# The first context tile in halves, the first weights one by one, the identity on ScalarE's queue, and twelve transposes on TensorE while it waits

## The chip, the core and the metric

The kernel runs on one core of a Trainium2 chip. A core has a matrix engine (TensorE, PE in the profile), VectorE (DVE), ScalarE (ACT), GpSimd (POOL) and SyncE (SP), which here only issues transfers; 16 DMA engines carry these. The metric is the time of one execution on the device in microseconds, as the median of several runs. The kernel before takes 2266.22 us (three runs: 2265.88, 2266.22, 2270.08).

## What is computed

One transformer layer on x [8, 256, 1024] and a context ctx [8, 256, 1024], in float32: cross attention with 32 query heads, 8 key and value heads and a rotary embedding, then a feed-forward product whose 4-bit weights are unpacked and scaled.

```python
q = rope(layernorm(x) @ Wq)                 # 32 heads of 128
k, v = rope(ctx @ Wk), ctx @ Wv             # 8 heads of 128, repeated 4 times
attn = softmax(where(mask == 0, -1e9, q @ k.T / sqrt(128)))
x = x + (attn @ v) @ Wo
x = x + layernorm(x) @ dequantize(qweight, qzeros, scales) + bias
```

## The kernel before

**Products in parts.** Each float32 operand is split into a high part (a copy rounded to the matmul's format, made by ScalarE) and a low part (operand minus high part, made by VectorE or GpSimd). A product of two operands is then three matmuls: high by high, high by low, low by high. They are lines 242, 243 and 244, in the helper `products`, so most of TensorE's work stands on these three lines.

**Stages.** Values and keys are made first, in 64 units of 24 matmuls (8 slices of the contraction, three matmuls each), for each half of the batch, and written to DRAM. Attention follows, pair of heads by pair of heads, with the output products by Wo behind it in a scheme with fewer multiplications, and the feed-forward product ends the kernel. The order of the work is written out by hand for each engine; engines meet only in semaphores, and each engine's instructions run in the order in which they stand.

**The start.** The first unit, `value_unit(V_H0_N0)` in the program of TensorE, multiplies context tile 0 by the value weights. Tile 0 is 128 partitions by 8 slices of 128 columns (512 KB, in `scores`, which serves as a ring of two buffers, `cring`). The weights are four pieces of two slices each (512 KB each, `wv_raw[0]` to `wv_raw[3]`, in the buffers `wraw` and `xring`). Unit 0 goes through the 8 slices, i = 0 to 7; before each even i it waits for another weight piece.

- SyncE issues, in this order: the identity (line 295), context tile 0 (`load_ring(0)`, line 306), the four weight pieces (line 340), context tile 1 (line 306), the positions (line 342), then further context tiles. A third tile goes into the first buffer of the ring and waits until VectorE has made tile 0's low part (`c_lo`).
- ScalarE copies tile 0 into `act_t` (`ring_hi`, line 854), the four weight pieces into `q_t` (line 910), then tile 1.
- VectorE subtracts for each of them (line 1132 for tiles, line 1220 for weights), then works out the table indices and goes on with the tiles.
- TensorE waits for the identity (`ident_in`), for tile 0's low part (`c_lo` 1) and for the first weight piece's low part (`wv_lo` 1), and starts unit 0. The identity is first used much later, by the transposes of the gathered table (`table_fill`, line 631) behind unit 4.
- GpSimd gathers the table for the rotary embedding, once VectorE has the indices (line 1531).

The semaphores that the start uses are `c_in` (a tile's landing), `wv_in` (a weight piece's landing), `c_hi` and `wv_hi` (ScalarE's copies), `c_lo` and `wv_lo` (VectorE's low parts), and `kv_done` (a finished unit).

Of the kernel before, what the change touches and what calls it, by code (L numbers as in the profile page):

```python
# [7 lines left out]
ALU = mybir.AluOpType  # L8
ACT = mybir.ActivationFunctionType
F32 = mybir.dt.float32  # L10
# [5 lines left out]
P = 128  # L16
# [31 lines left out]
BK_S, BK_Q, BK_T, BK_O = (0, 4), 2, 4, 6  # L48
# [21 lines left out]
def build(nc, x, ctx_t, x_tiles, x_pieces, pos, mask, wq, wk, wv, wo, qweight, qzeros, scales, bias, table, ident, out):  # L70
# [4 lines left out]
    with ExitStack() as stack:  # L75
        def sem(name):
            return stack.enter_context(nc.semaphore(name))
# [5 lines left out]
        def sb(name, shape, dt):  # L83
            return stack.enter_context(nc.sbuf_tensor(name, shape, dt))

        identity = sb("identity", [P, P], F32)
# [11 lines left out]
        ps = stack.enter_context(nc.psum_tensor("ps", [P, 8, NW], F32))  # L98
# [43 lines left out]
        act_v = act_t[:, :].rearrange("p (l k t) -> p l k t", l=2, k=KT)  # L142
        wv_parts = q_t[:, :].rearrange("p (k l c) -> p k l c", k=KT, l=2)
# [11 lines left out]
        cring = [scores[:, i * E:(i + 1) * E].rearrange("p (k c) -> p k c", k=KT) for i in range(2)]  # L155
        cring_wv = [scores[:, i * E:(i + 1) * E].rearrange("p (a c) -> p a c", a=2) for i in range(2)]
        gathered = scores[:, 2 * E:4 * E].rearrange("p (t c) -> p t c", t=TT)
        wv_raw = [b[:, :].rearrange("p (a c) -> p a c", a=2) for b in (*wraw, *xring)]
# [24 lines left out]
        x2t = [a_parts[:, i, :, :].rearrange("p l (k t) -> p l k t", k=KT) for i in range(2)]  # L183


        ident_in, pos_in, mask_in = sem("ident_in"), sem("pos_in"), sem("mask_in")
        c_in = [sem(f"c_in{i}") for i in range(2)]
        wv_in = [sem(f"wv_in{i}") for i in range(4)]
# [17 lines left out]
        out_stored = sem("out_stored")  # L206

        c_hi, c_lo, wv_hi, wv_lo = sem("c_hi"), sem("c_lo"), sem("wv_hi"), sem("wv_lo")
        w_hi, w_lo = sem("w_hi"), sem("w_lo")
        kv_done, kv_hi, kv_lo = sem("kv_done"), sem("kv_hi"), sem("kv_lo")  # L210
        k_rot, k_sum = sem("k_rot"), sem("k_sum")
# [26 lines left out]
        def products(eng, dst, left, right, ks, first, last):  # L238
            for k in ks:
                lh, ll = left(k)  # L240
                rh, rl = right(k)
                eng.matmul(dst, lh, rh, start=(k == first), stop=False)  # L242
                eng.matmul(dst, lh, rl, start=False, stop=False)  # L243
                mm = eng.matmul(dst, ll, rh, start=False, stop=(k == last))  # L244
            return mm
# [46 lines left out]

        @block.sync
        def _(sp):
            sp.dma_start(identity[:, :], ident).then_inc(ident_in, 16)

            def load_ring(item):
                if item >= 2:
                    sp.wait_ge(c_lo, item - 1)
                if C_WV1 <= item < C_H1:  # L300
                    sp.dma_start(cring_wv[item % 2], wv[1, item - C_WV1]).then_inc(c_in[item % 2], 16)
                elif item >= C_WV0:
                    sp.dma_start(cring_wv[item % 2], wv[0, item - C_WV0]).then_inc(c_in[item % 2], 16)
                else:
                    t = item if item < TT else item - C_H1 + TT
                    sp.dma_start(cring[item % 2], ctx_t[t]).then_inc(c_in[item % 2], 16)
# [28 lines left out]
                sp.dma_start(x_tile[t % 4], x_tiles[t]).then_inc(x_in[t % 4], 16)  # L335


            load_ring(0)
            for a in range(4):
                sp.dma_start(wv_raw[a], wv[0, a]).then_inc(wv_in[a], 16)  # L340
            load_ring(1)
            sp.dma_start(idx[:, :], pos).then_inc(pos_in, 16)
# [49 lines left out]
            for u in range(16):  # L392
                g = u // 2
                if u % 2 == 0:
                    i = KVH + g + 2
# [196 lines left out]
        def _(pe):  # L592
# [3 lines left out]
            def kv_bank(k):  # L596
                if k >= 4:
                    if is_value(k - 4):
                        pe.wait_ge(kv_lo, k - 3)
                    else:  # L600
                        pe.wait_ge(k_rot, keys_before(k - 4) + 1)
                return ps[:, BK_KV[k % 4], :]

            def value_unit(k, items=None, first=False):
                t = k % TT
                bank = kv_bank(k)
                for i in range(KT):
                    if first and i % 2 == 0:
                        pe.wait_ge(wv_lo, i // 2 + 1)
                    if items is not None and i % 2 == 0:  # L610
                        pe.wait_ge(c_lo, items + i // 2 + 1)
                    mm = products(pe, bank, lambda i: [act_v[:, l, i, t * P:(t + 1) * P] for l in range(2)],
                                  lambda i: [wv_parts[:, i, l, :] for l in range(2)], [i], 0, KT - 1)
                mm.then_inc(kv_done, 1)
# [9 lines left out]
            def table_fill(f):  # L624
                half = f // 4
                pe.wait_ge(table_in, (half + 1) * 16 * TT)
                if f >= 2:
                    pe.wait_ge(tb_cos, f - 1)
                    pe.wait_ge(tb_sin, f - 1)
                for i in range(4):  # L630
                    mm = pe.transpose(ps[:, BK_T + f % 2, i * P:(i + 1) * P],
                                      gathered[:, 2 * (f % 4) + i // 2, (i % 2) * P:(i % 2 + 1) * P], identity[:, :])
                mm.then_inc(tb_done, 1)

            for t in range(TT):
                pe.wait_ge(c_lo, t + 1)
                value_unit(V_H0_N0 + t, first=(t == 0))
                if t >= 4:
                    table_fill(t - 4)
            for u in range(16):  # L640
                key_unit(K_H0 + u, u // 2)
            for t in range(TT):
                value_unit(V_H0_N1 + t, items=C_WV1 if t == 0 else None)
                if t == 2:

                    pe.wait_ge(ln_ready, 1)
                    pe.transpose(ps[0:2 * TT, BK_Q, 0:P], mean_var[:, :, 0], identity[:, :])
                    pe.transpose(ps[0:2 * TT, BK_Q, P:2 * P], inv_std[:, :], identity[:, :]).then_inc(moments_turned, 1)
            for t in range(TT):
                pe.wait_ge(c_lo, C_H1 + t + 1)  # L650
                value_unit(V_H1_N1 + t)
                if 2 <= t < 6:
                    table_fill(t + 2)
# [186 lines left out]

        @block.scalar
        def _(act):
            def ring_hi(item):
                act.wait_ge(c_in[item % 2], (item // 2 + 1) * 16)
                if C_WV1 <= item < C_H1 or item >= C_WV0:
                    a = item - (C_WV1 if item < C_H1 else C_WV0)

                    act.wait_ge(kv_done, V_H0_N0 + TT if item < C_H1 else V_H1_N1 + TT)
                    act.activation(wv_parts[:, 2 * a:2 * a + 2, 0, :], cring_wv[item % 2], ACT.Copy).then_inc(c_hi, 1)
                    return  # L850
                t = item % TT if item < TT else item - C_H1
                if item >= C_H1:
                    act.wait_ge(kv_done, V_H0_N1 + t + 1)
                act.activation(act_v[:, 0, :, t * P:(t + 1) * P], cring[item % 2], ACT.Copy).then_inc(c_hi, 1)
# [49 lines left out]
                act.activation(next_rows(i, 0), next_raw[i % 4], ACT.Copy).then_inc(next_hi, 1)  # L904


            ring_hi(0)
            for a in range(4):
                act.wait_ge(wv_in[a], 16)
                act.activation(wv_parts[:, 2 * a:2 * a + 2, 0, :], wv_raw[a], ACT.Copy).then_inc(wv_hi, 1)  # L910
            ring_hi(1)
            for t in range(TT):
                if t + 2 < TT:
                    ring_hi(t + 2)
                if t in (4, 5):
                    head_hi(t - 4, 16)
                value_hi(V_H0_N0 + t)
                if t > 0:
                    store_unit(t - 1)
                if t >= 4:  # L920
                    table_cos(t - 4)
# [197 lines left out]
        def _(dve):  # L1119
            chain = [0]  # L1120

            def ring_lo(item):
                dve.wait_ge(c_hi, item + 1)
                if C_WV1 <= item < C_H1 or item >= C_WV0:
                    a = item - (C_WV1 if item < C_H1 else C_WV0)
                    dst, hi, src = (wv_parts[:, 2 * a:2 * a + 2, 1, :], wv_parts[:, 2 * a:2 * a + 2, 0, :],
                                    cring_wv[item % 2])
                else:
                    t = item % TT if item < TT else item - C_H1
                    dst, hi, src = (act_v[:, 1, :, t * P:(t + 1) * P], act_v[:, 0, :, t * P:(t + 1) * P],  # L1130
                                    cring[item % 2])
                dve.tensor_tensor(dst, src, hi.bitcast(F32), ALU.subtract).then_inc(c_lo, 1)
# [81 lines left out]
                                  ALU.not_equal).then_inc(mask_ready, 1)  # L1214


            ring_lo(0)
            for a in range(4):
                dve.wait_ge(wv_hi, a + 1)
                dve.tensor_tensor(wv_parts[:, 2 * a:2 * a + 2, 1, :], wv_raw[a],  # L1220
                                  wv_parts[:, 2 * a:2 * a + 2, 0, :].bitcast(F32), ALU.subtract).then_inc(wv_lo, 1)
# [486 lines left out]
```

## Time and profile before

| what | value |
|---|---|
| median of three runs | 2266.22 us (2265.88 to 2270.08) |
| the profiled execution's own time | 2266.87 us |
| its span | 2265.1 us |
| TensorE busy | 2227.8 us, 98% |
| VectorE, ScalarE, GpSimd busy | 61%, 47%, 61% |
| granted TensorE clock, mean | 0.996 of full speed |

The profiled execution is one run beside the three; its span runs from the first to the last instruction, and 1.8 us lie around it. Times in the rows are microseconds from the span's start. In a timeline the columns are start, duration, engine, line, operation, tiles written and read, shape, count, and in brackets the idle time of the engine before it with what ended it. A matmul's duration includes its way through the array, so neighbours overlap: the rate is read from the distance between two starts.

### The profile page before, as it was taken

The page shows a single profiled execution, that of the slowest core. Times are in us where ns is not written, and L with a number is a line of the kernel's source. Part 1 is how long each engine was busy: PE and PEld are TensorE (multiplying, and loading weights), DVE is VectorE, ACT ScalarE, POOL GpSimd, SP SyncE. Part 2 cuts the span into 40 slices and gives each one's busy share as a digit, 9 for nine tenths or more (in the row PEclk, how much of TensorE's full clock was granted, in tenths as well). Part 3 has the DMA queues.
Part 4 walks back from the last instruction along what each step waited for, and adds up shares of the span by engine and source line. Part 5 has one row for each costly group of instructions (what it writes and reads, how often), then busy time and mean ns, then how long its engine had stood idle before and what let it go on. Part 6 is the DMA issues. An engine that isn't in the chain of part 4 may idle for free.

```text
span 2265.1 us, 33277 instructions
## 1 busy us (share of the span) xinstructions
PE 2227.8 (98%) x10562; PEld 1867.3 (82%) x10562; DVE 1373.1 (61%) x2535; ACT 1057.5 (47%) x2296; POOL 1388.6 (61%) x981
## 2 busy tenths in 40 slices
PE   8999999999999999999999999899999999999999
PEld 6888888788888888788888888678888888888887
DVE  4772574777777778877777777522876345453532
ACT  3232133666667767666766666522333323331000
POOL 1320553688888889788888888665564363364210
PEclk9999999999999999999999999999999999999999
DMA  6766674777788888877877878587564454452111
GB/s 247 272 225 220 237 250 176 219 243 242 253 247 243 248 247 258 257 248 238 254 245 248 243 249 259 164 310 268 183 202 153 162 186 165 150 187 82 47 47 47
DMA packets 299757, 476.72 MB, mean 210 GB/s; under 512 B 23553, under 2 KB 195873, under 8 KB 299681
## 3 DMA queue, kind: packets, MB, share of 16 engines
q1 hardware_dynamic: 285600, 440.12, 60.3%
q10 hardware_dynamic: 13312, 33.56, 3.7%
q0 software_dynamic: 768, 2.10, 0.2%
q8 instruction: 39, 0.64, 0.1%
q14 instruction: 38, 0.30, 0.0%
HBM read 303.70 MB, written 171.98 MB: 210 GB/s over the span
## 4 chain that ended last, share of the span: by engine, by line
PE 85%; DMA 4%; POOL 3%; DVE 3%; SPq 2%; ACT 2%; issue 1%; ACTq 0%; POOLq 0%; DVEq 0%
PE ps L242 20%; PE ps L243 20%; PE ps L244 20%; PE ps L792 8%; PE ps L793 8%; PE ps L794 8%; DMA sq_scratch<-scores 3%; SPq L444 1%; POOL q_t L1596 1%; POOL rope_tmp L1536 1%; PE ps L816 1%; ACT probs L970 1%; POOL s_buf L1536 0%; DVE rows L1431 0%; DMA pt_raw<-sq_scratch 0%
## 5 line engine op out<-in xcount | busy, mean ns | idle before, releaser
L242 PE MATMUL ps<-act_t,wq_t 128*128 128x512 f32 x1280 | 501.7, 392 | 1.2 <-DVE wq_t L1136 0.6
L243 PE MATMUL ps<-act_t,wq_t 128*128 128x512 f32 x1280 | 501.0, 391 | 0.0
L244 PE MATMUL ps<-act_t,wq_t 128*128 128x512 f32 x1280 | 499.4, 390 | 0.0
L1614 POOL TENSOR_TENSOR b_parts<-wraw,b_parts 128x512 fp32r<-128x512 f32 x112 | 197.7, 1766 | 262.7 <-ACT b_parts L1010 262.7
L792 PE MATMUL ps<-b_parts,a_parts 128*128 128x512 f32 x896 | 349.3, 390 | 2.8 <-POOL b_parts L1614 1.3
L1596 POOL TENSOR_TENSOR q_t<-pt_raw,q_t 128x1024 fp32r<-128x1024 f32 x124 | 300.3, 2422 | 82.2 <-ACT q_t L988 80.3
L794 PE MATMUL ps<-b_parts,a_parts 128*128 128x512 f32 x896 | 348.7, 389 | 0.0
L793 PE MATMUL ps<-b_parts,a_parts 128*128 128x512 f32 x896 | 348.6, 389 | 0.0
L1315 DVE TENSOR_TENSOR a_parts<-xring,a_parts 128x1024 fp32r<-128x1024 f32 x112 | 149.6, 1335 | 306.9 <-ACT a_parts L1005 306.9
L1005 ACT ACTIVATE a_parts<-xring 128x1024 fp32r<-128x1024 f32 x112 | 118.7, 1060 | 391.8 <-PE ps L794 387.3
L1536 POOL TENSOR_TENSOR rope_tmp<-rope_tmp 128x512 f32<-128x512 f32 x144 | 193.4, 1343 | 150.6 <-DVE rope_tmp L1147 149.9
L244 PEld LDWEIGHTS ps<-act_t,wq_t 128*128 128x128 f32 x1280 | 241.2, 188 | 51.3
L242 PEld LDWEIGHTS ps<-act_t,wq_t 128*128 128x128 f32 x1280 | 241.7, 189 | 50.3 <-DVE act_t L1208 1.8
L243 PEld LDWEIGHTS ps<-act_t,wq_t 128*128 128x128 f32 x1280 | 241.6, 189 | 45.2
L970 ACT ACTIVATE probs<-scores,neg_max 128x256 f32<-128x256 f32 x512 | 253.9, 497 | 11.2 <-DVE neg_max L1304 11.0
L1145 DVE TENSOR_TENSOR rope_tmp<-ps,rope 128x512 f32<-128x512 f32 x144 | 99.4, 690 | 210.4 <-PE ps L244 192.9
L980 ACT ACTIVATE probs<-probs,inv_sum 128x256 f32<-128x256 f32 x512 | 216.9, 495 | 2.1 <-DVE inv_sum L1311 2.1
L962 ACT ACTIVATE q_t<-rope_tmp 128x512 fp32r<-128x512 f32 x128 | 81.1, 634 | 290.1 <-POOL rope_tmp L1536 290.1
L792 PEld LDWEIGHTS ps<-b_parts,a_parts 128*128 128x128 f32 x896 | 168.2, 188 | 40.1 <-issue 3.7
L1585 POOL TENSOR_TENSOR q_t<-rope_tmp,q_t 128x512 fp32r<-128x512 f32 x128 | 197.9, 1546 | 5.2 <-ACT q_t L962 5.2
L794 PEld LDWEIGHTS ps<-b_parts,a_parts 128*128 128x128 f32 x896 | 168.2, 188 | 35.2
L793 PEld LDWEIGHTS ps<-b_parts,a_parts 128*128 128x128 f32 x896 | 168.2, 188 | 34.4
(133 smaller groups left out, 4373.6 us busy)
## 6 DMA issues: line engine op xcount, KB each, us to landing
sq_scratch<-scores SPq DMA_DIRECT2D x124, 512.0 KB, 4.8
pt_raw<-sq_scratch SPq DMA_DIRECT2D x496, 128.0 KB, 3.1
xring<-left_scratch SPq DMA_DIRECT2D x112, 512.0 KB, 3.9
left_scratch<-s_buf SPq DMA_DIRECT2D x64, 640.0 KB, 4.9
wraw<-in_L_xattn_Wq SPq DMA_DIRECT2D x64, 512.0 KB, 4.7
wraw<-in_L_xattn_Wo SPq DMA_DIRECT2D x64, 512.0 KB, 4.8
v_scratch<-kv_t ACTq DMA_DIRECT2D x32, 512.0 KB, 3.2
k_scratch<-kv_t ACTq DMA_DIRECT2D x32, 512.0 KB, 4.9
```

The source lines that it names most:

```text
L242: eng.matmul(dst, lh, rh, start=(k == first), stop=False)
L243: eng.matmul(dst, lh, rl, start=False, stop=False)
L244: mm = eng.matmul(dst, ll, rh, start=False, stop=(k == last))
L792: pe.matmul(dst, lh, rh, start=(begins and not onto), stop=False, skip_group_check=True)
L793: pe.matmul(dst, lh, rl, start=False, stop=False, skip_group_check=True)
L794: mm = pe.matmul(dst, ll, rh, start=False, stop=ends, skip_group_check=True)
L970: e = act.activation(probs[:, par, j, qt, :], score_v[:, par, j, qt * S:(qt + 1) * S], ACT.Exp, bias=neg_max[:, par, j, qt:qt + 1], scale= ...
L980: e = act.activation(probs[:, par, j, qt, :], probs[:, par, j, qt, :], ACT.Copy, scale=inv_sum[:, par, j, qt:qt + 1])
L1536: pool.tensor_tensor(tmp[:, 0, :], tmp[:, 0, :], tmp[:, 1, :], ALU.add).then_inc(done, 1)
L1585: pool.tensor_tensor(q_parts[:, c, j, 1, :], rope_tmp[:, 0, :], q_parts[:, c, j, 0, :].bitcast(F32), ALU.subtract).then_inc(q_lo, 1)
L1596: pool.tensor_tensor(lo, pt_raw[:, u8 % 2, :], hi.bitcast(F32), ALU.subtract).then_inc(pt_lo, 1)
L1614: pool.tensor_tensor(b_parts[:, s % 2, 1, :], wraw[s % 2][:, 0:NW], b_parts[:, s % 2, 0, :].bitcast(F32), ALU.subtract).then_inc(right_lo, 1)
```

## The change

The transfer of the identity is issued by ScalarE at the start of its program, and no longer by SyncE. Context tile 0 is loaded, copied and subtracted in two halves of four slices each, with semaphores of their own (`first_in[0]`, `first_in[2]`); the first weight piece is loaded, copied and subtracted slice by slice (`first_in[1]`, `wv_in[0]`). SyncE's order is now: half tile, weight slice 0, weight slice 1, half tile, three whole weight pieces, tile 1. TensorE, once the identity has landed, transposes it twelve times into a bank that is not used until unit 4, then waits for `first_lo` 2 (first half tile and weight slice 0), before i = 1 for weight slice 1, before i = 2 for the second weight piece as before, and before i = 4 also for the second half tile. The counts on `c_in[0]` in `ring_hi` are lower by one landing, since tile 0 no longer counts there.

```diff
@@ sync @@
-            sp.dma_start(identity[:, :], ident).then_inc(ident_in, 16)
...
-            load_ring(0)
-            for a in range(4):
+            sp.dma_start(cring[0][:, 0:4, :], ctx_t[0, :, 0:4, :]).then_inc(first_in[0], 16)
+            sp.dma_start(wv_raw[0][:, 0, :], wv[0, 0, :, 0, :]).then_inc(first_in[1], 16)
+            sp.dma_start(wv_raw[0][:, 1, :], wv[0, 0, :, 1, :]).then_inc(wv_in[0], 16)
+            sp.dma_start(cring[0][:, 4:8, :], ctx_t[0, :, 4:8, :]).then_inc(first_in[2], 16)
+            for a in range(1, 4):
                 sp.dma_start(wv_raw[a], wv[0, a]).then_inc(wv_in[a], 16)
@@ tensor @@
                 for i in range(KT):
-                    if first and i % 2 == 0:
+                    if first and i == 0:
+                        pe.wait_ge(first_lo, 2)
+                    elif first and (i == 1 or i % 2 == 0):
                         pe.wait_ge(wv_lo, i // 2 + 1)
+                    if first and i == 4:
+                        pe.wait_ge(c_lo, 1)
...
+            for i in range(12):
+                pe.transpose(ps[:, BK_T, 0:P], identity[:, :], identity[:, :])
             for t in range(TT):
-                pe.wait_ge(c_lo, t + 1)
+                if t > 0:
+                    pe.wait_ge(c_lo, t + 1)
                 value_unit(V_H0_N0 + t, first=(t == 0))
@@ scalar @@
+            act.dma_start(identity[:, :], ident).then_inc(ident_in, 16)
...
-                act.wait_ge(c_in[item % 2], (item // 2 + 1) * 16)
+                act.wait_ge(c_in[item % 2], (item // 2 + item % 2) * 16)
...
-            ring_hi(0)
-            for a in range(4):
+            act.wait_ge(first_in[0], 16)
+            act.activation(act_v[:, 0, 0:4, 0:P], cring[0][:, 0:4, :], ACT.Copy).then_inc(first_hi, 1)
+            act.wait_ge(first_in[1], 16)
+            act.activation(wv_parts[:, 0, 0, :], wv_raw[0][:, 0, :], ACT.Copy).then_inc(first_hi, 1)
+            act.wait_ge(wv_in[0], 16)
+            act.activation(wv_parts[:, 1, 0, :], wv_raw[0][:, 1, :], ACT.Copy).then_inc(wv_hi, 1)
+            act.wait_ge(first_in[2], 16)
+            act.activation(act_v[:, 0, 4:8, 0:P], cring[0][:, 4:8, :], ACT.Copy).then_inc(c_hi, 1)
+            for a in range(1, 4):
@@ vector: the four subtractions in the same order, then @@
-            ring_lo(0)
-            for a in range(4):
+            for a in range(1, 4):
```

## Rows read from the trace of the kernel before

**Rows 1.** The page: TensorE's busy time, share of the span, instructions.

```profile
PE 2227.8 (98%) x10562; PEld 1867.3 (82%) x10562; DVE 1373.1 (61%) x2535; ACT 1057.5 (47%) x2296; POOL 1388.6 (61%) x981
```

**Rows 2.** TensorE's waits, whole run: us in total, times, longest.

```profile
PE ps L242 <- DVE q_t L1220: 9.2, 1, 9.2
PE ps L242 <- POOL q_t L1596: 6.7, 4, 2.2
```

**Rows 3.** TensorE's waits from 10 to 360 us, all of them.

```profile
PE ps L242 <- DVE wq_t L1136: 0.6, 2, 0.4
```

**Rows 4.** Timeline of SyncE's queue at the start.

```profile
0.76 0.40 SPq L295 DMA_DIRECT2D identity<-in_identity  x1
1.21 0.41 SPq L306 DMA_DIRECT2D scores<-in_ctx  x1
```

**Rows 5.** Timeline of ScalarE, 0 to 18 us.

```profile
0.76 1.28 ACT L854 ACT_TABLE_LOAD   x1 [0.76 <-PEq L1698]
5.46 1.06 ACT L854 ACTIVATE act_t<-scores 128x1024 fp32r<-128x1024 f32 x1 [3.42 <-DMA scores<-in_ctx]
6.74 1.06 ACT L910 ACTIVATE q_t<-wraw 128x1024 fp32r<-128x1024 f32 x1 [0.22 <-DMA wraw<-in_L_xattn_Wv]
8.01 1.06 ACT L910 ACTIVATE q_t<-wraw 128x1024 fp32r<-128x1024 f32 x1 [0.22 <-DMA wraw<-in_L_xattn_Wv]
...
11.87 1.06 ACT L854 ACTIVATE act_t<-scores 128x1024 fp32r<-128x1024 f32 x1 [0.24 <-DMA scores<-in_ctx]
...
17.79 0.60 ACT L866 ACTIVATE kv_t<-ps 128x512 fp32r<-128x512 f32 x1 [3.56 <-PE ps L244]
```

**Rows 6.** Timeline of VectorE, 0 to 19 us.

```profile
6.55 1.23 DVE L1132 TENSOR_TENSOR act_t<-scores,act_t 128x1024 fp32r<-128x1024 f32 x1 [6.55 <-ACT act_t L854]
7.82 2.50 DVE L1220 TENSOR_TENSOR q_t<-wraw,q_t 128x1024 fp32r<-128x1024 f32 x2
...
18.41 0.69 DVE L1141 TENSOR_TENSOR kv_t<-ps,kv_t 128x512 fp32r<-128x512 f32 x1 [2.60 <-ACT kv_t L866]
```

**Rows 7.** Timeline of TensorE's matmuls in unit 0 and unit 1's first.

```profile
9.20 0.77 PE L242 MATMUL ps<-q_t,act_t 128*128 128x512 f32 x1 [9.20 <-DVE q_t L1220]
9.76 0.63 PE L243 MATMUL ps<-q_t,act_t 128*128 128x512 f32 x1
...
15.28 0.40 PE L244 MATMUL ps<-q_t,act_t 128*128 128x512 f32 x1
...
17.59 0.39 PE L242 MATMUL ps<-q_t,act_t 128*128 128x512 f32 x1
```

**Rows 8.** Stretches: busy of PE, PEld, DVE, ACT, POOL; clock, DMA share, GB/s.

```profile
1430.00:1432.00 2.00, 0.00 (x0) 0.00 (x0) 1.97 (x8) 0.22 (x1) 2.00 (x2) 0.94 0.89 226
1432.00:1436.00 4.00, 3.91 (x15) 3.23 (x16) 0.94 (x4) 2.80 (x10) 3.78 (x4) 0.60 0.37 100
1452.00:1456.20 4.20, 3.85 (x15) 3.20 (x15) 1.12 (x3) 1.34 (x4) 1.09 (x1) 0.59 1.04 267
```

**Rows 9.** The same view of two stretches near the start.

```profile
5.00:10.00 5.00, 0.80 (x2) 0.74 (x3) 3.35 (x3) 3.87 (x4) 0.00 (x0) 1.00 1.03 417
...
24.00:28.00 4.00, 4.00 (x19) 3.31 (x18) 1.77 (x2) 0.79 (x1) 2.34 (x2) 1.00 1.04 354
```

**Rows 10.** DMA issues before 12 us: count, KB each, us to landing.

```profile
wraw<-in_L_xattn_Wv SPq DMA_DIRECT2D x2, 512.0 KB, 5.4
...
identity<-in_identity SPq DMA_DIRECT2D x1, 64.0 KB, 1.8
```

**Rows 11.** The chain, 0 to 60 us: four transposes of the table.

```profile
39.51 0.44 PE ps L631 x4
```

**Rows 12.** Timeline of TensorE around 1432 and 1439 us.

```profile
1432.09 0.77 PE L242 MATMUL ps<-q_t,kv_t 128*128 128x512 f32 x1 [2.21 <-POOL q_t L1596]
1432.65 0.63 PE L243 MATMUL ps<-q_t,kv_t 128*128 128x512 f32 x1
...
1439.33 0.47 PE L242 MATMUL ps<-q_t,kv_t 128*128 128x512 f32 x1 [1.80 <-POOL q_t L1596]
```

**Rows 13.** Timeline of GpSimd: the last of the eight gathers.

```profile
25.47 1.40 POOL L1531 DMA_INDIRECT scores<-in_rope_table,idx  x1 [0.30 <-issue]
```

More of the change, by code:

```diff
@@ L183, in build @@
         x2t = [a_parts[:, i, :, :].rearrange("p l (k t) -> p l k t", k=KT) for i in range(2)]
+        first_in = [sem(f"first_in{i}") for i in range(3)]
         ident_in, pos_in, mask_in = sem("ident_in"), sem("pos_in"), sem("mask_in")
@@ L208, in build @@
         c_hi, c_lo, wv_hi, wv_lo = sem("c_hi"), sem("c_lo"), sem("wv_hi"), sem("wv_lo")
+        first_hi, first_lo = sem("first_hi"), sem("first_lo")
         w_hi, w_lo = sem("w_hi"), sem("w_lo")
@@ L1214, in mask_bytes @@
                                   ALU.not_equal).then_inc(mask_ready, 1)
-            ring_lo(0)
-            for a in range(4):
+            dve.wait_ge(first_hi, 1)
+            dve.tensor_tensor(act_v[:, 1, 0:4, 0:P], cring[0][:, 0:4, :], act_v[:, 0, 0:4, 0:P].bitcast(F32),
+                              ALU.subtract).then_inc(first_lo, 1)
+            dve.wait_ge(first_hi, 2)
+            dve.tensor_tensor(wv_parts[:, 0, 1, :], wv_raw[0][:, 0, :], wv_parts[:, 0, 0, :].bitcast(F32),
+                              ALU.subtract).then_inc(first_lo, 1)
+            dve.wait_ge(wv_hi, 1)
+            dve.tensor_tensor(wv_parts[:, 1, 1, :], wv_raw[0][:, 1, :], wv_parts[:, 1, 0, :].bitcast(F32),
+                              ALU.subtract).then_inc(wv_lo, 1)
+            dve.wait_ge(c_hi, 1)
+            dve.tensor_tensor(act_v[:, 1, 4:8, 0:P], cring[0][:, 4:8, :], act_v[:, 0, 4:8, 0:P].bitcast(F32),
+                              ALU.subtract).then_inc(c_lo, 1)
+            for a in range(1, 4):
                 dve.wait_ge(wv_hi, a + 1)
```

## The prediction

> **What bounds the kernel now.** I read the page first. TensorE has something to do for 2227.8 us of a span of 2265.1 us, so 37.3 us of the span are all that any change to waits can touch [rows 1]. The list of TensorE's waits splits these: the longest single one by far, 9.2 us, stands before its first product, and the next entry is 6.7 us in four pieces [rows 2]. The same list cut to 10 to 360 us holds 0.6 us in two waits, so in all the stages behind the start TensorE runs without a break [rows 3]. What is saved before its first products therefore moves the rest forward as a block, unless something behind the start goes by another clock than TensorE's.
>
> The start is read engine by engine. SyncE issues the identity at 0.76 us and the first context tile at 1.21, the weights behind it [rows 4]. ScalarE copies the tile at 5.46 and then a piece each 1.28 us (6.74, 8.01 and so on to 11.87, six pieces with the first), each time 0.22 us after a landing, though one copy takes 1.06 us [rows 5]: it waits for bytes, and 512 KB take 1.28 us. VectorE follows with 1.25 us for each [rows 6]. So the path to the first product is issue, landing, 1.06 us, 1.23 us, start at 9.20 us. Then the reader is to look at the distances between starts in unit 0: 0.43 us for fourteen products, up to 15.28, then 0.23 us; the next unit begins at 17.59 [rows 7]. The same two distances stand beside recorded drops of the granted clock in the middle of the kernel, with 1.00 before and after, so 0.43 us is TensorE at 1.2 GHz and 0.23 us at 2.4 [rows 7, 8, 12]; the clock's column itself says 1.00 for the start, and I go by the distances. Unit 0 has thus two losses: it begins at 9.20, and 14 of its 24 products cost 0.20 us too much, 2.8 us.
>
> **The change part by part.** The identity leaves SyncE's queue: the first issue at 0.76 is now the tile's half. This moves that issue forward by 1.21 - 0.76 = 0.45 us; the bytes ahead of the later weights are the same ones, so these come between 0 and 0.45 us sooner. I take 0.2, since with 417 GB/s over 5 to 10 us the flow is full [rows 9]. ScalarE now issues 64 KB itself, 0.40 us at 0.76, before its table load of 1.28 us; both end near 2.5 us, before any data is there [rows 4, 5]. If the table load went first, the issue would be at 2.04.
>
> First product. Half a tile is half of 1.28, 0.64 us less flow: ready for ScalarE between 5.46 - 0.64 - 0.45 = 4.4 and 4.8, say 4.6. The first weight, the same bytes again, 5.25. A copy of 512 columns is 0.60 us [rows 5], a subtraction 0.69 us [rows 6]. 5.25 + 0.60 + 0.69 and the 0.13 us from VectorE's end to TensorE's start (9.07 to 9.20) give 6.7 us for the first product, 2.5 sooner. The second weight is ready by 7.3, the tile's second half by 7.9; both are needed later. The halves cost ScalarE 4 x 0.60 against 2 x 1.06 and VectorE 4 x 0.69 against 2 x 1.23, 0.3 us more for each, in gaps: both are free again by 7.9, and the third and fourth weights, whole as before, reach ScalarE only at 8.01 - 0.2 = 7.8. If that cover were gone, 0.3 us would go on the path.
>
> There is the catch: six products and then a pause. From 8.01 to the end of VectorE's second weight piece at 10.32 are 2.3 us [rows 5, 6], so the third weight is ready at 10.1 and its products start at 10.2. The first six take from 6.7 to 9.3 at 0.43 us, or to 8.1 at 0.23. The other 18 start at 10.2 in either case; the next pieces are ready at 11.4 and 12.7, ahead of them. **So the early start of six products is worth what it leaves over behind 10.2**, and the end of unit 0 hangs on the clock from there.
> The sum by the clock, against 17.59:
> - fast from 10.2 on: 10.2 + 18 x 0.23 = 14.3, gain 3.3 us;
> - slow from 10.2 for 3.4 us: 8 products to 13.6, 10 fast ones to 15.9, gain 1.65 us;
> - slow for 6.0 us: 14 slow ones, 4 fast ones to 17.1, gain 0.45 us.
> The 3.4 us are from two drops in mid-kernel: a mean of 0.60 over 4 us and 0.94 over the 2 before, between levels 1 and 0.5, is 3.2 + 0.24; 0.59 over 4.2 us is 3.4 [rows 8]. The 6.0 us are this kernel's own start, 9.20 to 15.2 [rows 7]. I take 3.4: it stands twice, and there too TensorE had worked a little before, while at the start it came from nothing. By the Trainium skill ("TensorE: Matmul & The Clock Gate", the clock gate section) slow is the idle state, and the number of slow matmuls at a start varies from run to run, so it should not be fitted. By that rule the runs of one binary would spread over the three ends above; the trace's 3.4 and 6.0 agree with it.
>
> The twelve transposes. Before, the identity landed 1.8 us after its issue [rows 10]; the same here gives 2.6 us, 3.8 if the table load goes first. Four transposes hold TensorE's chain for 0.44 us [rows 11], 0.11 each at the fast clock and 0.22 if twice that at the slow one. Twelve are 1.3 to 2.6 us, over by 5.3 at the latest (6.5 with the late issue), before 6.7. They cost nothing on the path while the first weight covers them; without that cover, 2.6. Whether they wake the clock no row shows: TensorE would rest from about 5 to 6.7 and again from 9.3 to 10.2. In mid-kernel a rest of 2.2 us ended at half clock, one of 1.8 us did not [rows 8, 12]. I give them nothing in the sum and keep 3.3 as the upper end.
>
> Pieces of 2 KB rows instead of 4 KB for 1 MB: not shown at the start. The bounds are 0 and the flow of 24 to 28 us, 354 against 417 GB/s, with other kinds of rows in it [rows 9]: 1048 KB in 2.96 instead of 2.51 us, 0.45 us. I take 0.1, inside the rounding: the copies' 1.28 us distance shows a stream whose transfers, though each took some 5.4 us to land, overlap [rows 5, 10].
>
> The waits added. On TensorE the wait for the first half and first weight stands ahead of everything, as the old one did. The one for the tile's second half (ready 7.9) stands before product 13, after 10.2. On SyncE the ring's third load waits for the tile's last subtraction: 7.9 against 7.8 now, nothing. Late next is unit 1's tile: copied at 11.87, subtracted by 14.2 [rows 5, 6], so ready at 14.0 to 14.2, just ahead of 14.3 in the best case. Unit 4's table transposes, at 39.5 now, need the last gather, whose issue starts at 25.47; with a landing of 5.4 us behind that it is there by 31 [rows 10, 11, 13], so 3 us less leave 5.
>
> **The sum:** 2266.87 (the profiled execution, 1.8 around its span) - 1.65 = 2265.2 us. The median shown is 2266.22, so 2264.6 us for it.
>
> **Rivals.** *The clock is awake at 10.2* (transposes plus six products are enough work). For it: the drops in mid-kernel end after 3.4 us of work, and from 6.7 this would be 10.1. Against: 6.0 at the start, and the pause. It gives 3.3, 2262.9 us.
> *The pieces come one behind the other.* If each small transfer adds its own landing, the identity's 1.8 us [rows 10], the tile's half comes at 4.6, the two weights at 6.4 and 8.2, the second half at 10.0, and the whole weights 1.28 us apart behind it, the last at 13.9. Its parts are ready 2.3 + 0.1 us later, and six products of 0.23 to 0.43 end unit 0 at 17.7 to 18.9: a loss of 0.1 to 1.3 us, 2266.9 us in the middle. Against it stand the landings that overlap in the rows. The Trainium skill ("DMA: Bandwidth & Descriptors", rules for kernel authors) has the rule that speaks for this rival, to coalesce small transfers because each carries a fixed cost; the same table says that an early issue hides that cost, and this trace agrees with the second.
> *Slower, by the pause.* The pause before the seventh product starts the slow time anew and more rests follow, so that TensorE runs at half clock through unit 1 as well: (18 + 24) x 0.43 from 10.2 is 28.3 us, against 17.59 + 24 x 0.23 = 23.1, a loss of 5.2, 2271.4 us. It decides only if the rise comes later than 17.1 us or so; nothing between 10.2 and 17 makes TensorE rest, so I hold it for unlikely.
> *A shift of 1 to 3 us shakes the attention.* Behind the start TensorE rests for 37.3 - 9.2 = 28 us in short pieces [rows 1, 2]; a few of them fall otherwise, 1 to 2 us to either side of the forecast, 2263 to 2266.6 us.
>
> **How the numbers follow.** Forecast case (slow from 10.2 for 3.4 to 6 us, gain 0.45 to 1.65, so 2264.6 to 2265.8 us) 0.48; clock awake 0.32; one behind the other 0.10; attention shaken 0.07; slower by the pause 0.03. A measurement of this kernel can tell about 0.2%, 4.5 us, from no change. The first two cases end within that: even 3.3 us is 0.15%. Faster by over 0.2% needs the best case and more than 1.2 us of luck: 0.08. Slower: 0.03. Same: 0.89. The range takes the awake case with 1 us of scatter at the low end, 2261.9, and no gain with 1 us at the high end, 2267.2; the runs shown reach from 2265.88 to 2270.08.
>
> **What would show it.** Right: twelve transposes before 6 us; a first product near 6.7; a rest of about 1 us before the seventh, released by VectorE's third weight piece; unit 1 starting between 15 and 17 us; later stages the same rows moved by that. Awake: 0.23 us between starts from 10.2. Wrong: a first product after 8 us, unit 1 waiting for its tile, a rest elsewhere before 360 us, or a gain above 3.5 us, which I have no source for.

## The result: slower by 0.17%, and the profile after

Over 21 executions of each, the changed kernel takes 2272.83 us (2266.67 to 2276.25) and the kernel before 2267.61 us (2264.82 to 2274.19): these are medians, 5.2 us apart. The ratio is 1.0017, with a 95% interval of 1.001 to 1.0025, and it is that of the means, which are 3.9 us apart (2272.19 and 2268.33). A second measurement (h3 below) gave 1.0011 (1.0 to 1.0022). The forecast was 2264.6 us. The three executions shown before the prediction had a median of 2266.22; with 21 it is 1.4 us higher, and one execution of the same program lies up to 9 us from another.

The profiled execution of the changed kernel took 2275.24 us, its span is 2273.4 us, 8.3 us more than before. TensorE's timeline at its start, the answer to [rows 7]:

```profile
4.30 2.82 PE L645 MATMUL ps<-identity 128*128 128x128 f32 x12 [4.30 <-DMA identity<-in_identity]
6.78 0.70 PE L244 MATMUL ps<-q_t,act_t 128*128 128x512 f32 x1
7.31 0.39 PE L245 MATMUL ps<-q_t,act_t 128*128 128x512 f32 x1
...
11.20 0.80 PE L244 MATMUL ps<-q_t,act_t 128*128 128x512 f32 x1 [2.54 <-DVE q_t L1253]
11.79 0.63 PE L245 MATMUL ps<-q_t,act_t 128*128 128x512 f32 x1
...
14.23 0.40 PE L245 MATMUL ps<-q_t,act_t 128*128 128x512 f32 x1
...
16.77 0.39 PE L244 MATMUL ps<-q_t,act_t 128*128 128x512 f32 x1
```

The last row is unit 1's first matmul, at 16.77 instead of 17.59. Against this one execution of the kernel before, the start gained 0.82 us. Note also that no rest stands between the transposes and the first product, while its last input was ready earlier. VectorE's timeline has the first weight's low part, which ends at 6.13 us:

```profile
5.44 0.69 DVE L1243 TENSOR_TENSOR q_t<-wraw,q_t 128x512 fp32r<-128x512 f32 x1
```

I then set the n-th matmul of one trace against the n-th of the other (leaving out the twelve transposes) and read how much later the changed kernel is:

```
stage where the matmul stands       time in before    after minus before
unit 1 begins                             17.6             -0.8
attention, first groups                  435.1             -1.0
attention, settled in its loop           597.8             +0.6
before the switch to the second half     873.6             +1.3
behind the switch                       1038.5             +3.8
before the end of the attention         1392.4             +4.6
behind it                               1508.9             +7.9
products by Wo, second scheme step      1647.6             +8.4
end                                     2260.9             +8.3
```

Up to 435 us the stream of TensorE is moved as a block, as forecast. The gain is lost in four short stretches: the attention's first groups, its switch, its end, and 0.5 us at a border of the output products. This is one pair of profiles, 8.3 us apart where the means are 3.9 apart, and not all of it repeats: in the second profile of the changed kernel (h3) the same four stretches take -0.8, +2.6, +1.4 and +2.1 us more than in the kernel before.

The list of TensorE's waits agrees with the first pair. The two rows that answer to the second of [rows 2] (its writer, line 1596, is line 1629 here) and to what stood just behind it:

```profile
PE ps L244 <- POOL q_t L1618: 12.5, 13, 2.7
PE ps L244 <- POOL q_t L1629: 5.0, 4, 1.9
```

The first of these was line 1585 in the kernel before:

```profile
PE ps L242 <- POOL q_t L1585: 5.9, 4, 2.4
```

TensorE waits 13 times for GpSimd's low parts of the queries (`query_lo`, line 1618) instead of 4 times.

### The profile page after: what moved, and what is told of

The parts are those of the page before. It is cut to its first block, busy times and chain, and to the rows that moved or that the text cites. A ratio compares the mean times of both kernels' runs of the same rounds, so it can differ in the third digit from the quotient of the medians.

```text
span 2273.4 us, 33307 instructions
## 1 busy us (share of the span) xinstructions
PE 2231.6 (98%) x10574; PEld 1867.8 (82%) x10574; DVE 1381.9 (61%) x2537; ACT 1058.4 (47%) x2298; POOL 1384.5 (61%) x981
## 4 chain that ended last, share of the span: by engine, by line
PE 69%; POOL 11%; DMA 7%; issue 5%; SPq 3%; DVE 3%; ACT 1%; POOLq 0%; ACTq 0%; DVEq 0%
PE ps L244 14%; PE ps L245 14%; PE ps L246 14%; PE ps L804 8%; PE ps L805 8%; PE ps L806 8%; DMA sq_scratch<-scores 5%; POOL q_t L1629 3%; POOL q_t L1618 2%; POOL rope_tmp L1569 2%; SPq L448 2%; DMA left_scratch<-s_buf 1%; POOL s_buf L1643 1%; POOL s_buf L1641 1%; POOL s_buf L1638 1%
```

## The experiments

Each kernel was measured beside the kernel before on one chip. The table has the ratio of the two with its 95% interval, and the shift of unit 1's first matmul against 17.59 in the one profiled execution. That shift holds chance as well: the three kernels whose start is that of the kernel before (increments, transposes ahead of the attention, transposes at the end) show -1.2, -1.3 and -1.2, so 17.59 was a late start. What differs is the clock: in unit 0 the kernel before has fourteen slow distances between starts, these three have nine, eight and seven. Their unit 1 begins at 16.31 to 16.40 us. Against that the changed kernel, with 16.77 us here and 18.40 us in its second profile, is 0.4 to 2.1 us late: **its start gains nothing.**

```
kernel                                executions  ratio    interval          unit 1, us
changed kernel, 1st time                  21      1.0017   1.001  to 1.0025    -0.8
changed kernel, 2nd time                  11      1.0011   1.0    to 1.0022    +0.8
e1  twelve transposes alone               12      1.0019   1.0006 to 1.0032    -1.1
e2  identity by ScalarE alone             12      1.0003   0.9992 to 1.0014    -2.2
e3  halves alone                          12      1.0003   0.9991 to 1.0015    +0.3
e4  changed, without the transposes       12      1.0011   0.9998 to 1.0025    -0.4
f1  24 increments at the start            12      1.0009   1.0    to 1.0018    -1.2
f2  twelve transposes before attention    11      1.0017   1.0006 to 1.0027    -1.3
f3  twelve transposes at the end          12      0.9994   0.9984 to 1.0003    -1.2
f4  24 transposes at the start            12      0.9995   0.9985 to 1.0006    -3.1
h4  the same again                        11      0.9997   0.9986 to 1.0009    -2.8
g1  128 small transposes, a                6      1.0037   1.0023 to 1.0051    +5.9
g1  the same, b                            5      1.0046   1.0033 to 1.0059    +6.0
g2  140 small transposes, a                5      1.0061   1.0048 to 1.0074    +8.7
g2  the same, b                            5      1.0064   1.0051 to 1.0077    +8.1
h1  changed, three products                6      1.003    1.0016 to 1.0044    -2.2
h2  before, three products                12      1.001    0.9997 to 1.0022    -1.7
```

0.001 is 2.3 us.

**First, one part at a time.** The four kernels are the kernel before with the transposes (e1), with the identity's issue moved (e2), with the halves (e3), and the changed kernel without its transposes (e4):

```diff
+            for i in range(12):                      # e1: into the kernel before
+                pe.transpose(ps[:, BK_T, 0:P], identity[:, :], identity[:, :])
             for t in range(TT):
                 pe.wait_ge(c_lo, t + 1)
```

> The kernel before with the twelve transposes alone, behind the wait for the identity. They begin near 2.6 us and are over by 5.5, before the first product at 9.2, so the start is where it was, or a few products are fast sooner (0 to 1 us gained in unit 0). Theory 'the shift upsets the attention' (its orbit depends on how the start of unit 0 stands to the other engines): nothing is shifted, so the median stays within 1.5 us of the kernel before. Theory 'the added instructions upset it' (24 more instructions ahead of TensorE's loops): the attention is about 5 us longer and the median about 2273.

> The kernel before with the identity issued by ScalarE's queue alone. The tile is issued 0.45 us sooner, so unit 0 starts 0 to 0.45 us sooner. Theory 'shift': at most a small effect, 0 to 2 us slower. Theory 'added instructions': ScalarE and SyncE each change by one transfer, TensorE by nothing: within 1.5 us of the kernel before. A third theory, that one more transfer on ScalarE's queue upsets later stores: about 5 us slower here.

> The halves and the first weights one by one, with the identity on SyncE's queue and no transposes. First products near 7.2 us, a rest before the seventh, unit 1 about 0.5 to 1 us sooner. Theory 'shift': the attention is 5 us longer, median about 2272. Theory 'added instructions on TensorE': TensorE has no more instructions than before, so the gain at the start is kept and the median is 2266 to 2268.

> The changed kernel without the twelve transposes. Theory 'shift': about as the changed kernel, 2271 to 2273. Theory 'added instructions on TensorE': the gain at the start is kept and nothing is lost behind it, 2265.5 to 2267.5 against 2267.6 before.

The transposes alone cost as much as the whole change, 1.0019, though unit 1 began 1.1 us early and TensorE waited for nothing inside unit 0. The halves and the identity's issue, each alone, cannot be told from no change. The changed kernel without its transposes lies between, at 1.0011, with an interval that reaches to 1. That speaks against "shift" as the whole cause: e1's start is where that of f3 below is (-1.1 and -1.2), and f3 costs nothing (the intervals do not meet).

**Second, is it the work or the instructions?**

```diff
             pe.wait_ge(ident_in, 16)
+            for i in range(24):                      # f1
+                hold(pe)                             # adds 1 to an unused semaphore
```

> The kernel before with 24 instructions that only add to an unused semaphore, ahead of TensorE's first product, in the place of twelve transposes with their twelve weight loads. No array work, no change at the start of unit 0. Theory 'layout' (24 more instructions ahead of the attention on TensorE move it against the pieces in which its program is fetched): about 4 us slower, as with the transposes. Theory 'early array work' (what the transposes do to the clock at the start): within 1.5 us of the kernel before.

> The kernel before with the twelve transposes directly ahead of the attention's first queries. They cost 12 x 0.11 = 1.3 us of TensorE. Theory 'layout': 1.3 + 4, some 5 us slower. Theory 'early array work': 1.3 us slower at most.

> The kernel before with the twelve transposes behind TensorE's last product, beside VectorE's last sum and the last store. Nothing ahead of any product changes. Both theories: within 1 us of the kernel before. It shows how far two kernels that are the same up to their last microseconds measure apart.

> The kernel before with 24 transposes at the start, from 2.6 to about 8 us. The clock is at 2.4 GHz when unit 0 begins at 9.2, so unit 0 takes 24 x 0.23 = 5.5 us instead of 8.4 and all that follows comes up to 2.9 us sooner. Theory 'layout': 48 instructions more, so again a loss of some us in the attention, or none if the alignment falls well. Theory 'early array work': a loss at least as large as with twelve, 4 us or more. Theory 'an earlier stream upsets the attention' (shift): a loss larger than with twelve.

24 increments that do nothing, ahead of a first matmul at its old place, cost 1.0009, about 2 us, with an interval that begins at 1.0: a small cost is likely, not shown. The transposes ahead of the attention cost 1.0017, 3.9 us, of which 1.3 are their own time. The control at the end measures 0.9994, which shows how far equal kernels come out apart. And 24 transposes at the start, twice the work of the twelve, cost nothing that can be told: 0.9995, and 0.9997 again later. So "early array work" falls by its own forecast: f2 has none of it and is slower, and f4 has twice as much and is not. The last one had the clock up for unit 0:

```profile
2.63 5.38 PE L636 MATMUL ps<-identity 128*128 128x128 f32 x24 [2.63 <-DMA identity<-in_identity]
8.81 0.47 PE L242 MATMUL ps<-q_t,act_t 128*128 128x512 f32 x1 [0.80 <-DVE q_t L1222]
9.12 0.39 PE L243 MATMUL ps<-q_t,act_t 128*128 128x512 f32 x1
9.35 0.39 PE L244 MATMUL ps<-q_t,act_t 128*128 128x512 f32 x1
```

The starts are 0.23 us apart from the second on (one of them 0.30), where the kernel before had 0.43 fourteen times [rows 7]. Unit 1 begins 3.1 and 2.8 us sooner, the earliest of all kernels tried, with none of the halves. Against the typical 16.3 to 16.4 us this is 1.5 to 1.9 us sooner, and some 1 us arrives at the end, less than the intervals.

**Third, whole pieces of program.** The profile's queue q8 carries pieces of 16384 bytes, 39 in the kernel before. With 256 or 280 instructions more on TensorE there are 40, so these are TensorE's program. If the place of the attention against these pieces were the cause, 256 instructions more would do nothing and 280 the same as 24. The kernels put 128 or 140 small transposes where f4 has its 24:

```diff
+            for i in range(128):                     # g1; 140 in g2
+                pe.transpose(ps[0:16, BK_T, 0:P], identity[:, 0:16], identity[:, :])
```

> The kernel before with 128 small transposes (16 columns loaded, 128 streamed) at the start, which are 256 more instructions on TensorE: exactly one of the 16 KB pieces in which its program is fetched, if an instruction is 64 bytes. The transposes take about 128 x 0.11 = 14 us from 2.6, unit 0 starts near 17 and at 2.4 GHz, and unit 1 near 22.5 instead of 17.6: 5 us later. Theory 'layout': the program stands to its pieces as before, so the median is 5 us above the kernel before and no more. Theory 'any change upsets the attention, with 24 or with 256 instructions': 5 + 3, about 8 us above it.

> The same with 140 small transposes, 280 more instructions: 24 past a full piece, and unit 1 about 1.3 us later than with 128. Theory 'layout': the loss of the twelve transposes comes back, 6.3 + 3, about 9 us above the kernel before and 4 above the one with 128. Theory 'no effect of the place': 6.3 us above the kernel before, 1.3 above the one with 128.

> The same kernel as g1_256_instructions_a a second time, for more executions: 5 us above the kernel before by 'layout', about 8 by 'any change'. The two also show how far one kernel measures from itself.

> The same kernel as g2_280_instructions_a a second time: about 9 us above the kernel before by 'layout', 6.3 by 'no effect of the place'.

The small transposes took 15.5 us for 128, so unit 1 began 6 us later, not 5, and 8 to 9 us later with 140. Times 2268 us, the ratios are 8.4 and 10.4 us for g1 and 13.8 and 14.5 us for g2. Beyond the delay, which should be taken from a typical start and not from 17.59 (1 us more), that leaves 1.5 to 3.5 us for g1 and 4 to 5 us for g2. The order is that of "layout", but g1 is not at zero; with 5 or 6 executions each, this does not settle it. That a later stream itself changes the attention is not excluded either.

**Fourth, the same work in fewer instructions.** Three products of the identity with itself stand in place of the twelve transposes, in the changed kernel (h1) and in the kernel before (h2). What they compute is not used.

```diff
-            for i in range(12):
-                pe.transpose(ps[:, BK_T, 0:P], identity[:, :], identity[:, :])
+            for i in range(3):
+                pe.matmul(ps[:, BK_T, 0:2 * P], identity[:, :],
+                          identity[:, :].rearrange("p (a c) -> p a c", a=1)
+                          .broadcast_to([P, 2, P]), start=True, stop=True)
```

> The changed kernel with three products of the identity with itself (256 columns) in the place of the twelve transposes: 6 instructions for 24, about the same 2.6 us of array work from 4.3 us on, so the start of unit 0 and of unit 1 is as in the changed kernel. Theory 'place of the program': with 18 instructions fewer ahead of the attention the loss is mostly gone, the median within 1 us of the kernel before. Theory 'array work or shift at the start': as the changed kernel, 3 to 5 us above the kernel before.

> The kernel before with the same three products from 2.6 us on, 6 instructions more. Theory 'place of the program': 0 to 1 us below the kernel before. Theory 'array work at the start': 4 us above it, as with the twelve transposes alone.

> The changed kernel once more, beside h1 on the same chip. 3 to 5 us above the kernel before, if the first measurement was not a matter of its chip.

> The kernel before with 24 transposes once more: unit 1 starts 2 to 3 us sooner than in the kernel before. Theory 'place of the program': 48 instructions cost less than 24, median 0 to 2 us below the kernel before. Theory 'array work': 2 us or more above it.

```profile
4.73 2.92 PE L645 MATMUL ps<-identity 128*128 128x256 f32 x6 [4.73 <-DMA identity<-in_identity]
...
11.12 0.51 PE L244 MATMUL ps<-q_t,act_t 128*128 128x512 f32 x1 [0.90 <-DVE q_t L1253]
```

This is h1, TensorE's timeline. Each product of the identity became two matmuls of 256 columns, so the three products are twelve instructions with their loads, not six. h1 has half of the added instructions and the highest ratio of the changed kernels, 1.003 (1.0024 by the means of its six executions; its interval overlaps those of the other two measurements). It is not within 1 us of the kernel before, as "place of the program" had it. h2 is at 1.001 with an interval that holds 1. So "24 instructions cost 4 us, fewer cost less" does not stand as a rule. What stands is that the changed kernel is slower in the first measurement and, by an interval that begins at 1.0, in the second (h3), and that 24 transposes are not (h4).

## Where the place of the program was seen to act

One spot shows a path from the place of TensorE's program to a wait of TensorE, and the same two outcomes in all 18 profiles. It is the last loss in the list, at 1634.6 us. The kernel before: the DMA queues and issues from 1626 to 1630 us, and then the timeline of VectorE, GpSimd and TensorE behind them:

```profile
q8 instruction: 1, 0.02, 2.2%
...
wraw<-in_L_xattn_Wo SPq DMA_DIRECT2D x1, 512.0 KB, 5.8
```

```profile
1632.67 1.21 DVE L1452 TENSOR_TENSOR w_parts<-dense,w_parts 128x1024 fp32r<-128x1024 f32 x1
...
1632.84 2.18 POOL L1626 TENSOR_TENSOR wraw<-wraw 128x512 f32<-128x512 f32 x1 [1.18 <-DMA wraw<-in_L_xattn_Wo]
...
1634.63 0.47 PE L792 MATMUL ps<-b_parts,a_parts 128*128 128x512 f32 x1 [0.79 <-DVE rows L1431]
```

The changed kernel at the same matmuls, the same two views:

```profile
wraw<-in_L_xattn_Wo SPq DMA_DIRECT2D x1, 512.0 KB, 4.7
```

```profile
1639.60 2.18 POOL L1659 TENSOR_TENSOR wraw<-wraw 128x512 f32<-128x512 f32 x1
...
1640.56 2.31 DVE L1485 TENSOR_TENSOR w_parts<-dense,w_parts 128x1024 fp32r<-128x1024 f32 x1
...
1643.61 0.47 PE L804 MATMUL ps<-b_parts,a_parts 128*128 128x512 f32 x1 [1.89 <-DVE rows L1464]
```

In the kernel before, a piece of TensorE's program (the q8 packet, 0.02 MB; 2.2% of 16 engines' 4 us is 1.4 us) is fetched while the load of `wraw` runs, and the load takes 5.8 us. GpSimd has to wait for it and starts after VectorE's subtraction has begun; that takes 1.21 us. In the changed kernel the piece was fetched some 300 matmuls earlier, the load takes 4.7 us, GpSimd starts first, and the same subtraction takes 2.31 us. VectorE's next operations free the banks that TensorE waits for, so it waits 1.1 us longer. The faster load makes the slower kernel. All five kernels with no instruction added ahead have the fetch there and 1.21 us; the eleven with 12, 24, 48 or 280 added have no fetch there, and 2.31 us; the two with 256 have the fetch, but 0.3 to 0.7 us sooner behind the load's issue, the load takes 5.3 to 5.6 us, and it is 2.31 us. A load of 5.7 us or more goes with the short subtraction and a shorter one with the long, 18 times of 18. That the fetch makes the load long is read from five profiles against eleven; no kernel moved the fetch alone.

What the order costs depends on the clock. In eight of the thirteen profiles with 2.31 us the longer rest (1.89 against 0.79 us) is followed within 2 us by a drop of the granted clock to half; after the shorter rest it is in none. Here f1, then the changed kernel, from the same matmul on (columns as in [rows 8]):

```profile
1644.50:1647.90 3.40, 3.40 (x10) 2.62 (x9) 3.40 (x6) 0.00 (x0) 1.28 (x1) 0.50 0.02 7
```

```profile
1645.10:1648.50 3.40, 3.40 (x17) 2.80 (x16) 3.40 (x6) 0.00 (x0) 1.29 (x1) 1.00 0.05 20
```

Ten matmuls at 1.2 GHz stand against 17 at 2.4. From 1630 to 1648 us of the kernel before, the eight with the drop take 2.1 us more than the kernel before, the five without it 0.5 us more, and the other kernels with no instruction added ahead 0.1 to 0.3 us less. So this one spot gives 0.5 to 2.1 us of the loss, f4 and h4 included.

The loss at the switch passes through a similar order of two engines, but I can't trace it to a fetch. The switch of the attention, GpSimd, the kernel before and the changed kernel:

```profile
877.92 0.74 POOL L1605 TENSOR_TENSOR s_buf<-o_buf 128x256 f32<-128x256 f32 x1 [0.21 <-DMA left_scratch<-s_buf]
...
879.31 2.28 POOL L1585 TENSOR_TENSOR q_t<-rope_tmp,q_t 128x512 fp32r<-128x512 f32 x1
```

```profile
882.19 1.65 POOL L1638 TENSOR_TENSOR s_buf<-o_buf 128x256 f32<-128x256 f32 x1 [1.35 <-DMA left_scratch<-s_buf]
...
884.48 2.24 POOL L1618 TENSOR_TENSOR q_t<-rope_tmp,q_t 128x512 fp32r<-128x512 f32 x1
```

GpSimd's sum waits for the store of the last sums, 0.21 us in one and 1.35 in the other. When it comes late it falls beside VectorE's subtraction and takes 1.65 instead of 0.74 us, and the query part behind it (line 1585, 1618) ends when TensorE already waits: 2.67 us there against none. Counted from one and the same matmul, in all 18 profiles, the sum starts between 4.1 and 5.3 us where TensorE does not wait for it, and between 5.5 and 7.3 us where it loses 1.4 to 2.8 us. Of the seven profiles with 24 or 280 instructions added ahead it is late in all but e1; it is also late in e4, g1 (a), h1 and f4, which add none, 256, 12 and 48, and early in g1 (b), h2 and h4, the last with the program of f4. So the same program falls on either side. From 873.6 to 1038.5 us the thirteen profiles with instructions added take 1.9 us more on average than the kernel before, the five without 0.2 us more. Why the store lands late is not shown.

## Why the prediction was wrong, step by step

**"A shift of 1 to 3 us shakes the attention", 1 to 2 us, mostly noise, with a chance of 0.07.** This is the step that failed, and with it the premise that what is saved before the first products "moves the rest forward as a block". The block was moved as forecast up to 435 us, but the attention's unsettled stretches took 8.9 us more in the profile (-1.0 to +7.9 in the list), while the whole kernel took 3.9 us more in the measured ratio. I read the idle time of one trace as if another execution would repeat it. By its span that trace was a lucky one, though its time, 2266.87 us, is only 0.7 us under the median of 21: of the five profiled kernels with no instruction added ahead, its span of 2265.1 us is the lowest, and the others have 2267.5, 2269.6, 2269.7 and 2272.2.

**The cost of the transposes, "nothing on the path".** This term was put at nothing on the ground that they are over before 6.7. They were not: the identity was there at 4.3 us (forecast 2.6, or 3.8 if its issue was late), so they ran from 4.30 to about 6.8, while the first weight's low part was ready at 6.13. The first product waited some 0.5 us for them, which cost nothing only because the seventh came at 11.20.

```profile
identity<-in_identity ACTq DMA_DIRECT2D x1, 64.0 KB, 3.5
```

Behind the start I had not counted that they lengthen TensorE's program ahead of all that follows. e1 shows a cost of 4.3 us (1.4 to 7.3), f1 that increments with no array work may have about half of that. The size is not a rule (h1, f4), and how much of it comes through fetches can be read at one spot only.

**The range.** It ended at 2267.2, below the kernel before's own median of 2267.61. Three executions with a spread of 4 us were too few for a range 5.3 us wide.

**The pieces' landings.** Forecast: 0 to 0.45 us for rows of 2 KB, the third weight 0.2 us sooner. ScalarE reached the weights' second piece, the first whole one, at 8.83 us, 0.8 later than the same piece at 8.01 [rows 5] and 1.0 later than forecast:

```profile
8.83 1.06 ACT L932 ACTIVATE q_t<-wraw 128x1024 fp32r<-128x1024 f32 x1 [0.64 <-DMA wraw<-in_L_xattn_Wv]
```

The flow from 5 to 8 us says why:

```profile
5.00:8.00 3.00, 3.00 (x14) 2.74 (x14) 1.82 (x3) 1.48 (x3) 0.00 (x0) 1.00 0.91 330
```

330 GB/s, against 415 in the same 3 us of the kernel before, while pieces with rows of 2 KB arrive. My lower bound for the flow, 354, was not low enough. The halves lose 0.8 us for all that follows, and more in e3, with the identity on SyncE (9.24 us, 1.2 later). e2, the identity's issue moved and nothing else, has this piece at 7.31 us, 0.7 sooner, so beside it the halves cost 1.5 us. The rival "one behind the other" was thus partly right, and the rule that speaks for it, to coalesce small transfers (the Trainium skill, "DMA: Bandwidth & Descriptors", rules for kernel authors), bore on the sum more than I let it: the flow, 330 against 415 GB/s, goes its way, though that rule's figure, 64 KB, is far below these pieces of 256 KB.

**The clock.** I gave the transposes nothing; in the trace they woke the clock. TensorE worked without a rest from 4.30, and from 7.31 on the starts are 0.23 us apart: the rival's step. But six fast products and a late weight make the rest 2.54 us, not 0.9, and the clock falls again. The view's clock over 10 to 14 us:

```profile
10.00:14.00 4.00, 2.80 (x7) 2.22 (x8) 3.82 (x4) 3.23 (x4) 0.00 (x0) 0.58 0.65 258
```

0.58 over 4 us is 3.4 us at 1.2 GHz, the very length of the drops in [rows 8]. Six of the 18 products behind the rest were slow. Unit 1 came at 16.77 us, inside the forecast's 15.9 to 17.1 but by luck: the 18 products began 1.0 us late, and fewer of them were slow than the eight to fourteen of the forecast. The second profile (h3) has a rest of 3.06 us, thirteen slow products and unit 1 at 18.40:

```profile
11.50 0.80 PE L244 MATMUL ps<-q_t,act_t 128*128 128x512 f32 x1 [3.06 <-DVE q_t L1253]
```

The kernel before itself has a longer drop than the two that I read the 3.4 us from:

```profile
916.35:923.20 6.85, 6.31 (x18) 4.67 (x17) 4.41 (x13) 3.83 (x11) 3.27 (x4) 0.50 0.95 268
```

So the gain of 1.65 us, too, was not there: it was counted against the one late start of 17.59. In h1 the six products were slow, the rest was 0.90 us and the products behind it were fast from the second on; unit 1 came at 15.4.

**What held:** a rest before the seventh product with VectorE as its releaser (2.54 us, not 1), and no wait between there and 360 us but the two of [rows 3]. The first product (6.7 forecast, 6.78 measured) is luck: its data was ready some 0.5 us sooner, and the late transposes held it back.

## What stays open

Why the changed kernel loses some 3 to 5 us is narrowed, not settled. Shown: in the profile the loss is in short stretches from 435 us on, of which the switch, the end and the border repeat in the second profile; the transposes alone bring a loss of this size (e1, f2); and it needs neither the halves nor an earlier stream. Strongly suggested by 18 profiles: the place where TensorE's program is fetched decides the order of the engines at the border. Not shown: that it needs no array work (f1's interval begins at no change), and that fetches decide the other stretches. Alignment alone does not order the kernels. Some of the differences between 17 ratios with intervals of 0.001 to either side will be chance.

No version tried beats the kernel before by more than the intervals. Of those that change the start, the 24 transposes with the old loads come nearest (0.9995 and 0.9997).

## What to carry to other kernels

When an edit at the start gains one or two microseconds, look at the rest of the trace for stretches in which several engines run close together: their order can flip with a small change, and here that was worth more than the edit. Before counting a gain at the start, look at how far that start moves between executions: unit 1 began 1.3 us apart in kernels with the same start. Measure such an edit with some twenty executions of each kernel, since one lucky trace of the kernel before makes each change look like a loss. If TensorE is to be awake for its first products, give it work up to them and nothing that lets it rest long behind them: rests of 0.80 and 1.74 us ahead of the first product kept the fast clock in f4 and h4, rests of 2.54 and 3.06 us behind the sixth lost it in the changed kernel.

## What was unexpected of the hardware

- A 512 KB load took 5.7 to 5.9 us where a fetched piece of 16 KB program, 1.4 to 1.9 us long for the DMA that carries it, fell into it (five profiles), and 4.7 to 5.1 us where none did (eleven).
- A subtraction of 1024 columns on VectorE takes 1.21 us if it begins before GpSimd's sum and 2.31 us if it begins after it, 18 times of 18.
- ScalarE's starts on two pieces of 256 KB in rows of 2 KB were 1.28 us apart (6.28, 7.56), as they are for 512 KB in rows of 4 KB; in e3, e4 and h3 the same pieces were 1.5 to 2.1 us apart.
- Twelve transposes at the start took 2.48 us to the first product behind them, 0.21 each, against 0.11 in [rows 11].
